# Closing steps of a GNN layer: the final pair but one is summed on GpSimd, centred and scaled in one ScalarE operation, and multiplied by gamma on GpSimd

## The reference

```
n = tanh(linear(out, Wni, bni) + r * linear(hid, Wnh, bnh))
out = (1.0 - z) * n + z * hid
mu, var = mean(out), var(out)                    # over the 256 features
result = (out - mu) / sqrt(var + 1e-5) * gamma + beta
```

## Time and profile before

| what | value |
|---|---|
| median of 3 runs | 513.74 us (513.68 to 513.78) |
| the profiled execution's own time | 513.44 us |
| its span in the profile | 511.6 us |
| busy share: PE, DVE, ACT, POOL | 96%, 84%, 82%, 72% |

### The profile page before, as it was taken

How to read it: one execution, slowest core, us unless ns; L and a number is a source line. 1 busy time by engine, 2 the same in 40 slices (tenths; PEclk the granted TensorE clock), 3 DMA queues, 4 the chain that set the end, 5 groups by cost and what they waited for, 6 DMA issues and landing times.

```text
span 511.6 us, 10659 instructions
## 1 busy us (share of the span) xinstructions
PE 492.2 (96%) x2951; PEld 445.0 (87%) x2951; DVE 428.3 (84%) x1077; ACT 421.8 (82%) x819; POOL 367.8 (72%) x369
## 2 busy tenths in 40 slices
PE   8987899999999999999999999999999999999992
PEld 4776779999999999999999999999999999999892
DVE  4897789888888888888898888889888888988877
ACT  4857678888888888888888888888988889897772
POOL 2776867777877777787777778777777887775535
PEclk9999999999999999999999999999999999999997
DMA  8211121111222111122221112222111222110111
GB/s 291 109 54 42 41 84 52 53 56 59 74 74 72 59 57 45 54 72 72 72 71 48 54 42 72 72 72 72 51 51 41 72 72 72 51 41 22 42 42 62
DMA packets 20261, 33.42 MB, mean 65 GB/s; under 512 B 2256, under 2 KB 6992, under 8 KB 20240
## 3 DMA queue, kind: packets, MB, share of 16 engines
q1 hardware_dynamic: 19872, 32.38, 19.5%
q10 hardware_dynamic: 288, 0.52, 0.3%
q0 software_dynamic: 80, 0.26, 0.1%
HBM read 24.77 MB, written 8.39 MB: 65 GB/s over the span
## 4 chain that ended last, share of the span: by engine, by line
PE 84%; DVE 7%; POOL 3%; ACT 2%; issue 2%; DMA 1%; POOLq 0%; ACTq 0%; DVEq 0%
PE y_bank L411 24%; PE alpha L411 24%; PE gamma L411 12%; PE p_bank L448 11%; PE beta L411 10%; PE t_bank L456 2%; DMA shared<-in_wdT 1%; PE t_bank L437 1%; DVE y_lo L1232 1%; POOL wo_lo L1796 1%; DVE bias_step L1398 1%; DVE masks L1209 0%; DVE y_lo L1308 0%; POOL x_lo L1840 0%; POOL x_f L1788 0%
## 5 line engine op out<-in xcount | busy, mean ns | idle before, releaser
L448 PE MATMUL p_bank<-y_hi,masks 128*128 128x256 f32 x256 | 67.2, 284 | 3.0 <-issue 2.2
L448 PE MATMUL p_bank<-y_lo,masks 128*128 128x256 f32 x256 | 66.5, 282 | 0.0
L1910 POOL TENSOR_TENSOR x_lo<-x_f,x_hi 128x1024 fp32r<-128x1024 f32 x27 | 65.0, 2407 | 1.2 <-ACT x_hi L1044 1.2
L1913 POOL TENSOR_TENSOR y_lo<-shared,y_hi 128x512 fp32r<-128x512 f32 x28 | 36.5, 1303 | 25.0 <-ACT y_hi L1067 25.0
L448 PEld LDWEIGHTS p_bank<-y_hi,masks 128*128 128x128 f32 x256 | 48.1, 188 | 7.0 <-issue 4.1
L1899 POOL TENSOR_TENSOR var_eps<-mean_var,ln_eps 128x2 f32<-128x2 f32 x27 | 5.3, 195 | 65.4 <-DVE mean_var L1512 65.4
L448 PEld LDWEIGHTS p_bank<-y_lo,masks 128*128 128x128 f32 x256 | 48.2, 188 | 1.3
L411 PE MATMUL y_bank<-wd_hi,x_hi 128*128 128x512 f32 x112 | 46.8, 418 | 0.2 <-ACT shared L1052 0.2
L1015 ACT ACTIVATE p_bank<-p_bank,ratio 128x256 f32<-128x256 f32 x112 | 45.2, 446 | 0.1
L411 PE MATMUL y_bank<-wd_lo,x_hi 128*128 128x512 f32 x112 | 44.3, 396 | 0.0
L411 PE MATMUL y_bank<-wd_hi,x_lo 128*128 128x512 f32 x112 | 44.1, 394 | 0.0
(11 more groups left out here) (317 smaller groups left out, 1789.3 us busy)
## 6 DMA issues: line engine op xcount, KB each, us to landing
x_f<-in_xT SPq DMA_DIRECT2D x32, 256.0 KB, 2.6
x_rows<-in_x SPq DMA_DIRECT2D x32, 256.0 KB, 2.6
out<-shared SPq DMA_DIRECT2D x31, 256.0 KB, 2.0
adj_in<-in_adjT SPq DMA_DIRECT2D x32, 128.0 KB, 2.0
shared<-in_wgT SPq DMA_DIRECT2D x2, 576.0 KB, 6.2
shared<-in_wdT ACTq DMA_DIRECT2D x2, 256.0 KB, 5.1
vec_rows<-in_vectors SPq DMA_DIRECT2D x1, 512.0 KB, 6.3
shared<-in_wgT SPq DMA_DIRECT2D x2, 192.0 KB, 7.0
```

The lines of the kernel that those rows point to most:

```text
L448: last = nc.tensor.matmul(p_bank[:, b * H:(b + 1) * H], masks[:, k % 2, g, d, :], part[:, g, d * H:(d + 1) * H], start=first, stop=(part i ...
L1910: nc.gpsimd.tensor_tensor(*split_lo(x_lo[:, k % XRING, :, :], x_f[:, k % 2, :, :], x_hi[:, k % XRING, :, :])).then_inc(xlo_ready, 1)
L1913: nc.gpsimd.tensor_tensor(*split_lo(y_lo[:, EVEN, half(1)], u3_y[:, :], y_hi[:, EVEN, half(1)]))\
```

## The change

The sum of pair 30 moves from VectorE (PSUM `mix`) to GpSimd, which writes it to `late_rows`, a part of `shared` that an earlier stage (`u3_y`) has done with. VectorE takes mean and variance from there, later in its stream than before, and then computes `shift` = -mean * rstd (128 x 2) in one small operation. ScalarE computes rstd * row + shift in one operation for each graph. GpSimd then multiplies by gamma (new operation, 128x512) and, after `end_root(EVEN, 2)`, adds beta. The two `centre` operations of pair 30 on VectorE are gone. `end_mean` and `end_centre` of ODD stand before the statistics of pair 30, and `end_sum(EVEN, 1, 4)` after them.

```diff
--- before.py
+++ after.py
@@ -117,11 +117,14 @@
         end_pre = sides(scratch[:, 1024:1536])
         end_out = sides(scratch[:, 1536:2048])
         end_rn = out_rows
+
+        late_rows = sides(later(4608, 1))
         end_part = sides(o_sums[:, 0:4, :].rearrange("p b n -> p (b n)"))
         end_stats = sb("end_stats", [128, 2, 6])
         end_mv = sb("end_mv", [128, 2, 2])
         end_ve = sb("end_ve", [128, 2])
         end_rstd = sb("end_rstd", [128, 2])
+        shift = sb("shift", [128, 2])
         half_bias = sb("half_bias", [128, 512])
 
 
@@ -271,6 +274,8 @@
         late_r_ready = sem("late_r_ready")
         late_scaled = sem("late_scaled")
         late_ready = sem("late_ready")
+        shift_ready = sem("shift_ready")
+        late_gamma = sem("late_gamma")
         result_ready = sem("result_ready")
 
         def run_steps(eng, plain_step, step):
@@ -1195,7 +1200,12 @@
 
                 end_tanh(EVEN, 4)
                 end_gate((EVEN, 1), end_z_ready)
-                scale_norm(last - 1)
+
+                act.wait_ge(shift_ready, 1)
+                act.wait_ge(stored[(last - 1) % 2], 16 * ((last - 1) // 2))
+                for g in range(2):
+                    nc.scalar.activation(normed[:, (last - 1) % 2, g, :], late_rows[:, g, :], ACT.Identity,
+                                         bias=shift[:, g:g + 1], scale=rstd[:, g:g + 1]).then_inc(late_scaled, 1)
             head()
             run_steps(act, step, fast_step)
             tail()
@@ -1739,18 +1749,23 @@
                 dve.wait_ge(oslo_ready, last - 1)
                 dve.wait_ge(end_nh_ready, 1)
                 end_mixed(ODD, 1)
-                dve.wait_ge(late_scaled, 2)
-                mixed(last - 1)
                 end_stats_of(ODD, 1)
-                moments(last - 1)
                 end_hidden(EVEN, 0, 2, p_bank[:, 0:128])
                 end_sum(EVEN, 0, 3)
                 end_hidden(EVEN, 1, 2, end_nh)
-                end_sum(EVEN, 1, 4)
                 end_mean(ODD, 1)
                 end_centre(ODD, 1)
-                centre(last - 1, 0)
-                centre(last - 1, 1)
+
+                dve.wait_ge(mix_ready, last)
+                for g in range(2):
+                    nc.vector.bn_stats(stats[:, g, :], late_rows[:, g, :]).then_inc(stats_ready[g], 1)
+                for g in range(2):
+                    dve.wait_ge(stats_ready[g], last)
+                    nc.vector.bn_aggr(mean_var[:, g, :], stats[:, g, :]).then_inc(mv_ready, 1)
+                end_sum(EVEN, 1, 4)
+                dve.wait_ge(rstd_ready, last)
+                nc.vector.scalar_tensor_tensor(shift[:, :], mean_var[:, :, 0], -1.0, rstd[:, :], ALU.mult, ALU.mult)\
+                    .then_inc(shift_ready, 1)
                 end_mixed(EVEN, 2)
                 end_stats_of(EVEN, 2)
                 end_mean(EVEN, 2)
@@ -1971,13 +1986,21 @@
                 pool.wait_ge(result_ready, 2 * (last - 2))
                 root(last - 2)
                 mixing(last - 1)
-
-                pool.wait_ge(mix_ready, last)
+                pool.wait_ge(zpart_ready, last)
+                pool.wait_ge(yl22_ready, YPAIRS)
+                nc.gpsimd.tensor_tensor(late_rows, z_part[:, :].rearrange("p (g f) -> p g f", g=2),
+                                        n_sb[:, :].rearrange("p (g f) -> p g f", g=2), ALU.add).then_inc(mix_ready, 1)
                 add_beta(last - 2, 1)
+
                 root(last - 1)
                 end_root(ODD, 1)
+                pool.wait_ge(late_scaled, 4)
+                nc.gpsimd.tensor_tensor(normed[:, (last - 1) % 2, :, :], normed[:, (last - 1) % 2, :, :],
+                                        vec_rows[:, gamma_rows].unsqueeze(1).broadcast_to([128, 2, H]), ALU.mult)\
+                    .then_inc(late_gamma, 1)
+                end_root(EVEN, 2)
+                pool.wait_ge(late_gamma, 1)
                 add_beta(last - 1, 2)
-                end_root(EVEN, 2)
 
             head()
             run_steps(pool, step, fast_step)
```

## The result

The changed kernel takes 515.89 us (median of 7 runs, 515.03 to 516.19), the kernel before 513.64 us (7 runs, 513.37 to 513.78). The ratio on record is 1.0034, with a 95% interval of 1.0024 to 1.0043: slower by 0.34%. The profiled execution took 515.89 us, with a span of 514.1 us against 511.6 before.

The account below looks back on a forecast made before the run. It took VectorE's number of operations to set the kernel's end before the change. Late add_beta and three queued stores put the span at 513.0 against 511.6, so 513.74 + 1.4 = 515.1 us, range 514.5 to 515.9.

Parts of the forecast that it names:

- VectorE up to the statistics: Pair 30's statistics on VectorE start at 503.27, complete at 504.24, 0.90 us later; m marks ODD's first end_mixed operation.
- rstd and the wait: GpSimd finishes rstd at 505.32, so VectorE idles 0.99 us before shift starts at 505.43.
- `shift` blocked behind the power: Rival: GpSimd's power blocks VectorE's shift, everything from shift on 0.5 us later, 515.6 us; chance 0.20.
- ScalarE's pair: Pair 30's two ScalarE operations with SBUF input and bias take 0.88 us, between 0.84 and 0.98.
- the sign of a wrong step: On ScalarE, VectorE or GpSimd: pair over 1 us, shift over 0.5 us, or GpSimd's sum holding the statistics.
- gamma, root, beta: On GpSimd, gamma ends at 507.88, EVEN's root follows, then add_beta(30, 2) runs 508.62 to 509.88.
- The three stores: On SP, pair 30's store and both of pair 31's issue in a row; span ends 3.1 us after T.
- T: Time when SP issues the first of its last three stores, released by add_beta(30, 2), forecast at 509.90.
- overlap better: Rival on the last stores: only their issues count, T + 2.8 and T 0.1 earlier, 514.7 us; chance 0.10.
- The sum: Whole span: 513.0 us against 511.6, 1.4 us longer, giving a median of 515.1 us.

Follow-up runs that it names:

- e5: Changed kernel, VectorE only negating pair 30's mean and GpSimd multiplying it by rstd into shift; from ODD's first end_mixed operation to span end 13.18 us, against 13.11.
- e8: As e4, but pair 30's statistics right behind end_stats_of(ODD, 1), where they stood before the change; tail 11.68 us, against 11.54 in the kernel before.
- e7: Changed kernel with ScalarE's two operations as Copy with scale alone, no bias; the two took 0.91 us against 1.09, tail 12.91 us.
- e1: Kernel before, with only add_beta(30, 2) moved behind end_root(EVEN, 2); median 516.30 us, ratio 1.0038 to before, tail 13.15 us.
- e2: Changed kernel with add_beta(30, 2) back ahead of end_root(EVEN, 2); median 515.11 us, ratio 1.0020, tail 12.74 us.
- e3: Changed kernel with pair 31's two stores ahead of pair 30's store on SP; median 515.23 us, ratio 1.0020, tail 12.31 us.
- e9: As e4, but pair 30's statistics ahead of ODD's end_mean and end_centre; median 513.63 us, ratio 0.9990 to the kernel before, tail 10.88 us.
- e4: Changed kernel keeping the sum on GpSimd and VectorE's new order, but pair 30's mean, gamma, scale and beta as before; 513.35 us, ratio 0.9988, tail 11.08 us.

## Why the prediction was right, and where it was off

**VectorE up to the statistics**: right, to 0.02 us (statistics at m + 3.17 forecast, m + 3.19 measured; complete at m + 4.14 and m + 4.15). The sum on GpSimd was hidden, as said, done at m + 2.54.

**rstd and the wait**: right. Root at m + 4.24 forecast, m + 4.23 measured. `shift` started at m + 5.23 where I had m + 5.33: the signal from GpSimd took 0.03 us, not the 0.11 that I read before the last `end_normal`. The idle time was 0.90, not 0.99. That the wait gives back most of what VectorE saves is true of VectorE, and e5 shows that it is not what the kernel pays with.

**`shift` blocked behind the power**: didn't happen. It took 0.16 us, 506.23 to 506.39, though a GpSimd operation (`end_ve`, 506.17 to 506.36) ran beside it; the power began at 506.43, after it. So the rival's condition, a `shift` that comes while the power runs, was not met. A VectorE operation of that kind did come during a power in e8, the centring of pair 30, which there reads both `late_rows` and gamma's row from SBUF:

```profile
505.93 0.55 POOL L1970 TENSOR_TENSOR end_rstd<-end_ve,power 128x1 f32<-128x1 f32 x1
506.04 0.88 DVE L1765 SCALAR_TENSOR_TENSOR mix<-shared,mean_var,vec_rows 128x256 f32<-128x256 f32 x2
```

The pair took 0.88 us, against 0.87 before with one input in PSUM. So this power held nothing back. The forecast's price of 0.5 us for a blocked `shift` rested on an operation beside a much longer one, of 128x512, and no run here shows it beside a power.

**ScalarE's pair**: mis-sized. 0.88 forecast with 0.98 as the upper bound, 1.09 measured. It passes the bound, which came from VectorE's rows and not from an operation with a bias (e7), and it is over the 1 us that the forecast itself named as the sign of a wrong step.

**gamma, root, beta**: the mechanism was right, each term some 0.09 late with the pair; `add_beta` ended at m + 9.87, forecast m + 9.78. The last `end_normal` ended at m + 9.23, forecast m + 9.15, before m + 9.37: earlier than before, as said, and of no use to the end. That the last place of the addition is enough to make the end late is shown by e1; that gamma ahead of the root makes it late as well, by e2.

**The three stores**: T + 3.1 forecast, 3.2 measured, so they don't overlap better. e3 shows that their queueing behind pair 30's is worth 0.8.

**The sum**: 1.4 forecast for the tail, 1.6 measured, ScalarE's pair being the largest part of the difference. The measured medians differ by 2.25 us, since four of the seven runs have the 0.9 us of the lower clock, in a stage that the change doesn't touch; I had not seen this, for the trace of before didn't have it. The three runs without it, 515.03 to 515.31, are 1.4 to 1.7 over before's median. The median, 515.89, lies 0.01 inside the upper edge of the range, 515.9, by a cause that the range wasn't made for: that it lies inside is luck. That the change is slower by 1.4 to 1.7 us is not. Whether the change makes this fall of the clock more frequent the runs can't say: the streams are the same up to there, and runs of the kernel before have such times too; none of the 7 had them beside the changed kernel's 4 of 7. The runs beside the experiments were made on more than one chip, and the study doesn't tell chips apart. That remains open.

## What to carry to other kernels

When work is taken off the busiest engine of a closing sequence, follow the engine that receives it to its last instruction, and then to what waits in order behind it: in the kernel before, the addition moved behind the last root cost 1.6 us though it used no more time than before (e1). In the changed kernel half of the 1.6 us came from two finished results that stood behind its store on the same queue (e3). The parts don't add up: with gamma on GpSimd too, putting the addition back regained only 0.4 us (e2). An idle gap in the profile is a cost only if its engine's chain ends last; e5 removed a gap of 0.9 us and gained nothing. And a move to a slower engine pays if its result is needed only after other work: the same sum on GpSimd was worth 0.7 us (e9), 0.5 us (e4) or -0.1 us (e8), by the place of its reader.

## What the runs showed of the hardware

- ScalarE, two operations of 128x256: 0.84 us from PSUM with a scale, 0.91 us from SBUF with a scale, 1.09 us from SBUF with a scale and a bias, each of one number per partition.
- A VectorE operation with two SBUF inputs is not always held by GpSimd's. One of 128x4 took 0.85 us beside an operation of 128x512 and ended with it, at 23.24 against 23.23. In e8 one of 128x256 began 0.11 us into a power of 128x1 and was not held: 0.88 us for the pair, as without it. The Trainium skill, SBUF — State Buffer, section "Who interferes with whom", has the later one blocked until the other ends; the first row agrees, e8 doesn't. `shift` itself decides nothing: it took 0.16 us and ended 0.03 us after the operation of 0.19 us beside it, so a block could hide in its own duration, and spans on GpSimd are rough. In the other direction GpSimd's power for rstd took 0.79 us in e4, where it began during VectorE's centring with both inputs in SBUF, and 0.70 us in the changed kernel, where VectorE was idle: 0.09 us more. Held until the centring ended, at 505.47, it would have ended near 506.2, an estimate from these figures; it ended at 505.62.
- The issue of a store on SP took 0.33 to 0.34 us alone and 0.43 to 0.45 us when another was issued just before it.
- TensorE's granted clock fell to 1.2 GHz for some 3 us near 53 us in some executions of the same program and not in others, after a stretch in which TensorE was busy for 0.46 us of 2; in e3 it was busy for 0.32 us of that stretch and the clock didn't fall. The fall moved the rest of the program by some 0.9 us, more than half of what the change under study costs.
